# One fused transformer block: two PSUM bank sets for the last attention unit, and a new order of the steps before the router

## The reference

```python
h = layernorm(x) * (1 + ca) + sa
x = x + ga * attention(h)                       # causal, 16 heads
h = layernorm(x) * (1 + cb) + sb
scores = sigmoid(h @ gate_w.T)
topk_score, topk_ids = top_k(scores.T, 512)     # 16 experts over all 4096 tokens
eo = (silu(xin @ gw + gb) * (xin @ up + up_b)) @ down + down_b      # F = 1024
shared = (silu(h @ sh_gate) * (h @ sh_up)) @ sh_down                # SH = 512
x = x + gb * (scatter(eo * topk_score) + shared)
```

## Time and profile before

| | |
|---|---|
| median of 3 runs | 1237.21 us (1232.77 to 1240.11) |
| the profiled execution | 1228.18 us, its span 1226.5 us |
| mean granted clock of TensorE | 0.958 |
| busy: PE, DVE, POOL, ACT | 91%, 70%, 52%, 49% of the span |
| last unit of attention ends on PE | at about 447.9 us |
| first matmul of the experts | at about 629.8 us |

### The profile page before, as it was taken

The page is one execution under the profiler, slowest core; times in us unless marked ns, Lnnn a source line. Parts: engine busy times, 40 slices in busy tenths (PEclk is TensorE's granted clock), DMA queues, the critical chain, the costliest instruction groups (busy, mean ns, idle before and its releaser), DMA issues.

```text
span 1226.5 us, 21562 instructions
## 1 busy us (share of the span) xinstructions
PE 1120.3 (91%) x7422; PEld 875.4 (71%) x7422; DVE 858.3 (70%) x2174; ACT 600.0 (49%) x1085; POOL 642.5 (52%) x680
## 2 busy tenths in 40 slices
PE   4988988998898889999788999999999999999997
PEld 3545655555555457888677888888888888888886
DVE  5677797797786536778866776677776677776662
ACT  2247777776775563322143554444554444554441
POOL 4124476575573655222326666656666656666654
PEclk9679999999998789999999999999999999999998
DMA  5836768868778435875544445554545554556531
GB/s 168 104 51 112 110 123 169 168 134 173 142 141 161 140 104 181 205 202 145 159 127 116 144 123 159 126 133 116 145 124 158 126 130 119 145 122 160 126 87 18
DMA packets 100588, 165.46 MB, mean 135 GB/s; under 512 B 18680, under 2 KB 65272, under 8 KB 98432
## 3 DMA queue, kind: packets, MB, share of 16 engines
q1 hardware_dynamic: 84096, 137.86, 45.7%
q0 software_dynamic: 14336, 25.70, 10.9%
q10 hardware_dynamic: 2048, 0.53, 0.3%
HBM read 103.97 MB, written 34.13 MB: 113 GB/s over the span
## 4 chain that ended last, share of the span: by engine, by line
PE 34%; POOL 24%; issue 18%; DVE 9%; DMA 8%; SPq 3%; ACT 3%; ACTq 1%; POOLq 0%; DVEq 0%
POOL HTl L1642 12%; PE LB L761 6%; PE MB L761 6%; PE LB L505 4%; POOL out_y L1690 4%; PE MB L505 4%; POOL XG L1649 4%; DMA HT<-Us 3%; PE UB L505 3%; PE LB L598 3%; DVE junk L1167 3%; PE UB L614 2%; PE XB L505 2%; SPq L304 2%; DMA XT<-hD 2%
## 5 line engine op out<-in xcount | busy, mean ns | idle before, releaser
L1642 POOL TENSOR_TENSOR HTl<-HF,HTh 128x512 fp32r<-128x512 f32 x160 | 222.9, 1398 | 242.9 <-ACT HTh L973 242.7
L1167 DVE CUSTOM_DVE_ANT_0 junk<-MB,MK 128x256 bf16<-128x256 f32 (+3 forms) x512 | 219.8, 484 | 63.8 <-PE MB L575 62.4
L1553 POOL TENSOR_SCALAR_AFFINE_SELECT P<-P 128x256 f32<-128x256 f32 x256 | 101.4, 420 | 143.0 <-ACT P L913 143.0
L598 PE MATMUL LB<-QS,KS 50*128 50x256 f32 (+3 forms) x512 | 129.4, 372 | 16.2 <-ACT P L911 13.5
L973 ACT ACTIVATE HTh<-HF 128x512 fp32r<-128x512 f32 x160 | 100.4, 627 | 89.4 <-DVE HF L1429 89.4
L1690 POOL DMA_INDIRECT out_y<-EO,IDX x64 | 106.6, 1666 | 69.2 <-DVE EO L1516 63.7
L575 PE MATMUL MB<-KS,QS 48*128 48x256 f32 (+3 forms) x512 | 134.2, 377 | 8.0 <-DVE NM L1167 4.6
L911 ACT ACTIVATE P<-LB 128x768 f32<-128x768 f32 x128 | 103.8, 811 | 75.6 <-PE LB L598 75.1
L980 ACT ACTIVATE SIL<-LB,gbT 128x512 f32<-128x512 f32 x64 | 43.8, 685 | 185.4 <-PE LB L505 181.2
L598 PEld LDWEIGHTS LB<-QS,KS 50*128 50x128 f32 x512 | 83.2, 201 | 64.6 <-issue 46.5
L761 PE MATMUL LB<-WDh,HTh 128*128 128x256 f32 x320 | 94.3, 295 | 18.0 <-POOL HTl L1642 17.9
(11 more groups left out here) (265 smaller groups left out, 3011.1 us busy)
## 6 DMA issues: line engine op xcount, KB each, us to landing
WR<-in_gw SPq DMA_DIRECT2D x16, 1024.0 KB
WR<-in_uw SPq DMA_DIRECT2D x16, 1024.0 KB
WR<-in_dw SPq DMA_DIRECT2D x16, 1024.0 KB
QS<-ST SPq DMA_DIRECT2D x96, 128.0 KB, 4.8
KS<-ST SPq DMA_DIRECT2D x96, 128.0 KB, 5.9
hD<-h SPq DMA_DIRECT2D x8, 1024.0 KB, 5.5
XT<-hD SPq DMA_DIRECT2D x8, 1024.0 KB, 10.3
X<-in_x SPq DMA_DIRECT2D x8, 512.0 KB, 6.5
```

The lines of the kernel that those rows point to most:

```text
L598: m = e.matmul(LB[:, o:o + w], KS[base:base + 50, k, j * 128:(j + 1) * 128], QS[base:base + 50, k, 128 * j:512], start=True, stop=True)
L1167: m = e.tensor_tensor_reduce(junk[:, o:o + w], MB[:, o:o + w], MK[:, 512 - w:512], 1.0, -3e38, ALU.add, ALU.max, NM[:, k // 4, 4 * (k % 4) ...
L1553: m = e.affine_select(out=dd, in_=dd, compare_op=ALU.is_ge, fill=0.0, base=0, pattern=[[0, 2], [1, 128]], channel_multiplier=-1)
L1642: e.tensor_tensor(HTl[:, slot, :], HF[i][:], HTh[:, slot, :].bitcast(F32), ALU.subtract).then_inc(g_ht, 1)
```

## The change

1. In the last unit, odd heads use MB in place of LB (its maxima pass is over), so a head waits for the exp of the head two before.
2. SP issues the loads of the shared gate and up weights in unit 14 after head 1 (before: head 5), and their cuts on ACT and DVE go from unit 15, heads 2 to 5, to unit 14, heads 3 to 6.
3. Batch 6's output projection goes behind the last PV on PE and DVE. Its addition to X, batch 7's too, unit 15's normalise and low part, and the halves of shift2 for batch 6 (first half) and batch 7 (both) go from GpSimd to DVE.
4. On ACT, scale2 of batch 6 goes from before w = 0 to w = 2, behind unit 15's HNh. Batch 7's output projection and batch 6's h2T go to w = 3, batch 6's scores to w = 5, batch 7's h2T to w = 6 and its scores into the middle of w = 6, between the gate and the up matmuls.
5. The search starts at w = 7 instead of 10. SP spreads unit 15's inverses before it loads the down weight, and its stores follow the new order.

```diff
@@ -49,7 +49,7 @@
...
-W_TOPK = 10
+W_TOPK = 7
 W_PIECES = 42
...
@@ -392,7 +392,7 @@
...
                     stack(u + 2, 1)
-                if (u, k) == (NU - 2, 5):
+                if (u, k) == (NU - 2, 1):
...
@@ -427,10 +427,10 @@
...
         inverses(NU - 1)
+        spread_inverses(NU - 1)
...
         e.dma_start(WR[1][:, 0:1024].rearrange("p (k n) -> p k n", k=4), kn(sd)).then_inc(c_wr[1], 16)
-        spread_inverses(NU - 1)
         e.wait_ge(a_p, 2 * 8 * NU)
...
@@ -438,9 +438,9 @@
...
                 store_h2(NB - 2)
-            if w == 5:
+            if w == 4:
+                store_x2(NB - 1)
                 store_split(NB - 2)
-                store_x2(NB - 1)
             if w == 6:
...
@@ -455,9 +455,9 @@
...
                 load_gate_rows((w - 14) // 2)
-            if w == 4:
-                e.wait_ge(c_xd, 16 * (NB - 1))
+            if w == 8:
+                e.wait_ge(c_xd, 16 * NB)
                 e.dma_start(VR[:], cpos[:, 512:520]).then_inc(c_pos, 16)
...
@@ -586,16 +586,22 @@
...
         def main(u, k):
             base, n = 64 * (u % 2), n_head(u, k)
+            last = u == NU - 1
+            ps = MB if last and k % 2 else LB
+            if last and k == 1:
+                e.wait_ge(d_mx, 3 * 8 * NU)
+                e.wait_ge(a_nm, 2 * NU)
             if k % 4 == 0:
...
                     e.wait_ge(a_rows, 1)
-                elif j in (2, 0):
-                    e.wait_ge(a_p, 2 * (n - 1) + (2 if j == 0 else 1))
+                elif j in (2, 0) and not (last and k == 1):
+                    e.wait_ge(a_p, 2 * (n - (2 if last and k else 1)) + (2 if j == 0 else 1))
                 o, w = SPAN[j]
-                m = e.matmul(LB[:, o:o + w], KS[base:base + 50, k, j * 128:(j + 1) * 128],
+                m = e.matmul(ps[:, o:o + w], KS[base:base + 50, k, j * 128:(j + 1) * 128],
                              QS[base:base + 50, k, 128 * j:512], start=True, stop=True)
...
@@ -695,10 +701,12 @@
...
                         hT(b + 2, k - 5, ("hTa", "hTb")[k - 5])
-                    if k in (6, 7) and old:
+                    if k in (6, 7) and old and new:
                         outproj(b - 1, k - 6, ("outa", "outb")[k - 6])
...
         pv(NU - 1, 1, 1)
+        outproj(NB - 2, 0, "o0")
+        outproj(NB - 2, 1, "o1")
...
@@ -733,6 +741,14 @@
...
+        parts = [0]
+        def last_scores():
+            parts[0] += 1
+            if parts[0] == 2:
+                scores(NB - 1, "s0")
         def glu(n, m, wg, wu, xt, hook):
...
@@ -794,18 +810,17 @@
...
                 scores(NB - 3, "s2")
-            if w == 4:
+            if w == 3:
                 outproj(NB - 1, 0, "o0")
                 outproj(NB - 1, 1, "o1")
+                h2T(NB - 2, 0, "h1")
+                h2T(NB - 2, 1, "h0")
             if w == 5:
-                h2T(NB - 2, 0, "h0")
-                h2T(NB - 2, 1, "h1")
-                scores(NB - 2, "s0")
-            if w == 9:
-                h2T(NB - 1, 0, "h2")
-                h2T(NB - 1, 1, "h3")
+                scores(NB - 2, "s1")
+            if w == 6:
+                h2T(NB - 1, 0, "h0")
+                h2T(NB - 1, 1, "h1")
             if w == W_TOPK:
-                scores(NB - 1, "s1")
                 ticks[0] = -5
...
@@ -814,7 +829,7 @@
...
                     e.wait_ge(c_xt[b % 2], 16 * (b // 2 + 1))
-                glu(n_glu(b, i) - 1, i, shG, shU, XT[b % 2], tick)
+                glu(n_glu(b, i) - 1, i, shG, shU, XT[b % 2], last_scores if w == 6 else tick)
             else:
...
@@ -908,9 +923,10 @@
...
                 e.wait_ge(p_pv, (n - NP) // 4 + 1)
-            e.activation(P[n % NP][:, 512:1280], LB[:, 512:1280], ACT.Exp).then_inc(a_p, 1)
+            ps = MB if u == NU - 1 and k % 2 else LB
+            e.activation(P[n % NP][:, 512:1280], ps[:, 512:1280], ACT.Exp).then_inc(a_p, 1)
             e.wait_ge(p_mm, 2 * n + 2)
-            e.activation(P[n % NP][:, 0:512], LB[:, 0:512], ACT.Exp).then_inc(a_p, 1)
+            e.activation(P[n % NP][:, 0:512], ps[:, 0:512], ACT.Exp).then_inc(a_p, 1)
...
@@ -1047,27 +1063,27 @@
...
                         hT(b + 2, k - 5, ("hTa", "hTb")[k - 5])
-                if u == NU - 1 and 2 <= k < 6:
-                    cut(0, k - 2)
+                if u == NU - 2 and 3 <= k < 7:
+                    cut(0, k - 3)
         store_heads(NU - 1, 1)
         split_heads(NU - 2)
-        scale2(NB - 2, 0)
-        scale2(NB - 2, 1)
         for w, (kind, b, i) in enumerate(ORDER):
-            if w == 3:
+            if w == 2:
+                split_heads(NU - 1)
+                scale2(NB - 2, 0)
+                scale2(NB - 2, 1)
                 cut(1, 0)
                 cut(1, 1)
-                split_heads(NU - 1)
-            if w == 5:
-                h2T(NB - 2, 0, "h0")
-                h2T(NB - 2, 1, "h1")
-            if w == 6:
+            if w == 3:
+                h2T(NB - 2, 0, "h1")
+                h2T(NB - 2, 1, "h0")
+            if w == 4:
                 scale2(NB - 1, 0)
                 scale2(NB - 1, 1)
-            if w == 9:
-                h2T(NB - 1, 0, "h2")
-                h2T(NB - 1, 1, "h3")
+            if w == 6:
+                h2T(NB - 1, 0, "h0")
+                h2T(NB - 1, 1, "h1")
             if w == W_TOPK:
...
@@ -1284,7 +1300,7 @@
...
                         hT(b + 2, k - 6)
-                    if k == 7 and old:
+                    if k == 7 and old and new:
                         outproj(b - 1, 0, "outa")
...
@@ -1305,13 +1321,43 @@
...
                     e.tensor_tensor(GPl[:, :, 112:128], grv, GPh[:, :, 112:128].bitcast(F32), ALU.subtract).then_inc(d_gate, 1)
-                if u == NU - 1 and 2 <= k < 6:
-                    cut(e, 0, k - 2)
-        outproj(NB - 2, 1, "outb")
+                if u == NU - 2 and 3 <= k < 7:
+                    cut(e, 0, k - 3)
+        def add_x(b, i):
+            xs = X[:, b % 4, 2 * i:2 * i + 2, :]
+            e.wait_ge(d_tf, 2 * b + i + 1)
+            e.tensor_tensor(xs, xs, tf[:], ALU.add).then_inc(g_x2, 1)
+        def normalise(u):
+            e.wait_ge(c_us[0], 32 * (u + 1))
+            e.wait_ge(c_us[1], 32 * (u + 1))
+            e.wait_ge(c_hd[u % 2], 16 * (u // 2 + 1))
+            e.wait_ge(g_hn, u)
+            e.tensor_tensor(nf[:], HT[u % 2][:], DN[u % 2][:], ALU.mult).then_inc(g_nf, 1)
+        def split_heads(u):
+            e.wait_ge(a_hn, u + 1)
+            e.tensor_tensor(HNl[:, u % 2, :], nf[:], HNh[:, u % 2, :].bitcast(F32), ALU.subtract).then_inc(g_hn, 1)
+        def shift2(b, half):
+            ks = slice(2 * half, 2 * half + 2)
+            e.wait_ge(a_th, 2 * b + half + 1)
+            e.wait_ge(p_h2T, 2 * b)
+            e.wait_ge(c_tab, 16 * b)
+            kept(e.tensor_tensor(th[:, ks, :], th[:, ks, :], BT[b % 2][:, 2:3, :].broadcast_to([128, 2, D]), ALU.mult))
+            settled()
+            e.tensor_tensor(H2[:, ks, :], th[:, ks, :], BT[b % 2][:, 1:2, :].broadcast_to([128, 2, D]), ALU.add).then_inc(g_h2, 1)
+        outproj(NB - 2, 0, "o0")
+        add_x(NB - 2, 0)
+        outproj(NB - 2, 1, "o1")
+        inverses(NU - 1)
+        add_x(NB - 2, 1)
         stats2(NB - 2, 0)
...
         moments2(NB - 2)
-        inverses(NU - 1)
...
@@ -1431,33 +1477,31 @@
...
             if w == 1:
+                normalise(NU - 1)
+                split_heads(NU - 1)
                 scores(NB - 3, "s2")
-            if w == 3:
+            if w == 2:
+                shift2(NB - 2, 0)
                 cut(e, 1, 0)
                 cut(e, 1, 1)
-            if w == 4:
-                outproj(NB - 1, 0, "o0")
-                outproj(NB - 1, 1, "o1")
+            if w == 3:
+                for j in range(2):
+                    outproj(NB - 1, j, f"o{j}")
+                    add_x(NB - 1, j)
                 stats2(NB - 1, 0)
-            if w == 5:
-                h2T(NB - 2, 0, "h0")
-                h2T(NB - 2, 1, "h1")
-                scores(NB - 2, "s0")
                 stats2(NB - 1, 1)
                 moments2(NB - 1)
+                h2T(NB - 2, 0, "h1")
+                h2T(NB - 2, 1, "h0")
+            if w == 5:
+                shift2(NB - 1, 0)
+                shift2(NB - 1, 1)
+                scores(NB - 2, "s1")
             if w == 6:
-                e.wait_ge(a_th, 2 * NB - 1)
-                e.wait_ge(p_h2T, 2 * NB - 2)
-                e.wait_ge(c_tab, 16 * (NB - 1))
-                kept(e.tensor_tensor(th[:, 0:2, :], th[:, 0:2, :], BT[1][:, 2:3, :].broadcast_to([128, 2, D]), ALU.mult))
-                settled()
-                e.tensor_tensor(H2[:, 0:2, :], th[:, 0:2, :], BT[1][:, 1:2, :].broadcast_to([128, 2, D]),
-                                ALU.add).then_inc(g_h2, 1)
-            if w == 9:
-                h2T(NB - 1, 0, "h2")
-                h2T(NB - 1, 1, "h3")
+                h2T(NB - 1, 0, "h0")
+                h2T(NB - 1, 1, "h1")
+                scores(NB - 1, "s0")
```

(16 more changed lines are left out.)

## The result

The changed kernel is slower: 1245.62 us (median of 18 runs, 1238.34 to 1248.94) against 1232.67 us for the kernel before in the same session (18 runs, 1220.27 to 1240.11), a ratio of 1.011 (95% interval 1.0087 to 1.0133). A second session gave 1.0115 (1.007 to 1.0159). The profiled execution took 1245.97 us with a span of 1244.1 us. Forecast were 1239.0 us and "same". The forecast started from 1237.21 us, the median of three runs of the kernel before, and added some 2 us; against the 1232.67 us of 18 runs the change costs 13 us. So the miss is 11 us, and not the 6.6 that the two times suggest. The ratios leave out the few executions in a slower state, and differ from the quotient of the medians by up to 0.003.

The account below looks back on a forecast made before the run. PE was taken to bound the kernel, with under 12 us of removable idle time. Seven terms summed to +2.5 us on the profiled execution, 1239.7 us from the median, shaded to 1239; range 1231 to 1245 us.

Parts of the forecast that it names:

- Term 1: Unit 14: moving the shared gate and up weights' loads and cuts there costs +1.8 us; bounds 0.5 and 6.
- term 7: Low clock behind the new 2.75 us idle stretch before the last PV: +1.7 us; bounds 0 and 5.
- rival B: Slower: DVE and ACT in unit 14 stand behind a late WR (10.3 us landing): +9, 1246 us; chance 0.17.
- Term 2: Unit 15: with two bank sets, scores no longer wait for the previous head's exp: -0.4 us.
- Term 3: End of unit 15: batch 6's output projection behind the last PV leaves PE idle 2.75 us there: +2.4 us.
- Term 4: Before w2: SIL ahead of scale2 on ACT removes a 2.5 us wait and 1.7 us of low clock: -4.2 us.
- Term 5: Shared stage from w1: the order by need removes 2.6 us of waits and adds 5.6: +3.0 us; bounds 2.5 and 8.
- rival C: In w1: DN lands quickly, at 456.8, so added waits fall from 5.6 to about 3.3: 1237.4 us, "same"; chance 0.2.
- Term 6: Top-k search three steps earlier: HTl wait gone, tail net -0.4, gather's wait unchanged: -1.8 us.

Follow-up runs that it names:

- f1: Changed kernel with 60 unused matmuls in three PE waits (last PV, batch 6's first h2T, gather): 1236.92 us, against 1243.0 us for the changed kernel.
- g1: Changed kernel with VectorE's two down-weight cuts moved behind batch 6's h2T: 1242.37 us, 1.0098 of the kernel before.
- g2: Kernel before with only the two bank sets of the last unit added: ratio 1.0032 (0.9999 to 1.0066) to the kernel before.
- e3: Changed kernel with batch 6's output projection put back into heads 6 and 7 of unit 15: 1240.73 us, 1.0089 of the kernel before.
- e4: Changed kernel with three parts undone (search at w10, cuts in unit 15, projection in heads 6 and 7): 1236.04 us, 1.0036 of the kernel before.
- h2: Kernel before with unused matmuls in four PE waits (first SIL, PT, w40's up matmuls, gather): ratio 0.9999 (0.9967 to 1.0031).
- i1: Kernel before with the change's WR loads in unit 14, cuts two heads later than the change's: ratio 1.0040 (1.0013 to 1.0066).

## Why the prediction was wrong, point by point

The means of the two traces of each kernel, against the terms as they were put. The sum agrees within 1 us between two traces of a kernel; the single rows are rough, with up to 6.6 us between two traces:

| stretch | terms | forecast | measured |
|---|---|---|---|
| unit 14 | 1 | +1.8 | +6.8 (27.45 against 20.7) |
| unit 15 to w0 | 2, 3, 7 | +3.7 | +3.4 (30.05 against 26.7) |
| w0 to expert 0 | 4, 5, 6 | -3.0 | +3.5 (188.8 against 185.3) |
| experts | none | 0 | -0.1 |
| sum | | +2.5 | +13.4 |

**Term 1 failed, and most: +6.8 us where it had +1.8.** The place and the chain were right: WR late, ACT at the first cut, DVE behind it, PE at the transpose of the maxima. The size was not, for two reasons. The first is the time at which the loads go out, which was put "right behind the HT transfer of head 1", 6.7 us after unit 14's first exp (404.3 less 397.6). The waits in front of these loads, above all that for the last stack DMAs (`c_stack`), were not priced; WR lies in part on the space from which these read. The second is the low clock, for which the term had nothing. SP's rows of the second trace of the changed kernel show it:

```profile
401.81 1.87 SPq L304 DMA_DIRECT2D KS<-ST  x3
406.86 0.51 SPq L314 DMA_DIRECT2D HT<-Us  x1
410.53 0.39 SPq L400 DMA_DIRECT2D WR<-in_sg  x1
```

SP is through with HT at 407.4, waits 3.0 us for the last KS transfer and issues WR 3.2 us behind HT. In seven of the ten traces with this edit it stood 1.9 to 3.4 us there. In the other three, the first trace of the changed kernel, f1 and g1, the gap is 0.2, but HT itself was 0.7 to 2.0 us later. The loads left 7.6 us (408.98 less 401.4) and 9.3 us after that exp. The landing itself, 5 us in my sum, was 5.8 us. So the first cut came 13.3 and 15.1 us after unit 14's first exp, against 12.0 forecast. In unit 14 PE is idle 6.3 and 7.7 us in the two traces, against 3.2 and 2.5 before: +4.1 on the mean, near the 1.8 plus the 1.3 and 3.1 us by which the cut was late. The clock (counted as under term 7) cost 7.0 and 4.7 us there, against 5.1 and 1.7, which is +2.5, though chance is as large in it. The lower bound of the term, a landing in 3.7 us, stood on no row; the eight traces in which ACT waited for WR have 5.8 to 6.7. This is the mechanism of rival B, which had 0.17, but not its cause (a transfer of 8 us or more), and that its 1246 met the measured time is luck: it was +9 on a start 4.5 us too high, where +13 was measured, a good part of it behind unit 14. The Trainium skill's fit (DMA: Bandwidth & Descriptors, "Anatomy of one DMA"), made for GpSimd's path, would have put WR at 4.4 us as an estimate; the 5.8 us of SP's two loads are above it.

**Term 2, right.** Unit 15 hardly moves with the bank sets alone (g2).

**Term 3, right; term 7, right in its first part.** PE idles 2.65 us before the last PV (2.75 forecast), and the clock, at 1.00 in the 2.5 us ahead of this wait, falls with it, costing 2.1 us in that PV alone (4.49 less 2.36) where 1.7 stood for the stall. By the ratios e3 takes back 2.6 us.

**Term 4, right.** The wait for SIL is gone.

**Term 5, too low.** DN was used 4.05 us after its issue, between the 5.6 of the sum and the 2.65 of rival C; and still PE waited 4.7 and 0.7 us at tf, where I had 2.3 and 0.9. The chain on DVE was taken at 0.69 us an operation. The two pieces of shift2 took 1.73 and 1.65 us, while GpSimd did its own half in the same time. The low clock behind this wait was only in the bounds of term 7. From w0's to w10's first gate matmul PE takes 46.5 and 47.1 us, against 44.1 and 44.3, so terms 4 and 5 together are +2.6 instead of -1.2.

**Term 6, half right, and the second failure.** The HTl wait at w11 went (w10 to w12 takes 6.2 us instead of 7.5: -1.4, as forecast), PT's 2.4 and tb's 3.3 came where and as large as put. From w12 to w42 the changed kernel takes 102.7 and 102.9 us, the one before 103.3 and 110.0, the last by low clock. But "the gather for expert 0 stays at w42 and its wait stays" is wrong: it went from 3.5 to 7.84 us, and with the low clock behind it w42 to expert 0 takes 33.8 and 32.2 us instead of 27.0 and 26.9. I had moved VectorE's instructions and not looked at which of SP's transfers wait for them (GBt, XL, the store of `out_y`), and what meets the gather when they go out.

**Term 7, too small as a whole, and the third failure.** It charged the clock for one stall. Adding up (1 - clock) times PE's busy time over windows of 1 us, from w0 to expert 0, the clock cost 10.8 and 8.5 us in the changed kernel, 5.1 and 9.7 us in the one before. Of the mean difference of 3.5 us there, 2.3 is idle time and 2.3 the clock, less 1.1 of busy time elsewhere. The spread within one kernel is as large as the difference, so that single traces don't give the clock's share; f1's timed runs do, with 6 us for the clock behind its three places.

**What stays open.** e4's remainder of 0.0036 (it may be anything from 0.0003 to 0.0069) has no single step shown for it; the two bank sets, which it contains, gave 0.0032 (-0.0001 to 0.0066) alone. i1's 0.0040 has no stall in its trace that explains it. That the store of `out_y` lengthens the gather was not tested by moving it.

## What to carry to other kernels

When a load is moved ahead, price its own waits first: it can go no earlier than the last reader of the space it lands in, and the engines that stand in front of its data stop in order. When an engine's list is moved, follow which DMA issues wait for that list, and which large transfers then go out together with a small one that somebody waits for. And charge each long wait of PE with the low clock behind it: in this kernel every one of 2.6 us or more between w0 and expert 0 had it. Where such a wait can't be removed, a dozen unused matmuls in it can be cheaper than leaving it empty, as in f1; h2 shows that it need not be. Last, take two traces of a kernel before pricing a stretch of it.

## What the runs showed of the hardware

- The time goes with the granted clock from run to run. Over 133 runs of the kernel before, in five sessions, the mean clock went from 0.948 to 0.973 and the time from 1218.87 to 1241.61 us, with a correlation of -0.75, about 7 us per 0.01. The large waits behind w0 agree within 0.7 us between two traces of a kernel, except that for XT (1.0 and 2.7 us before); the falls of the clock don't. The Trainium skill (TensorE: Matmul & The Clock Gate, "What's actually happening") says that one kernel shows a different number of slow matmuls from run to run. It says so of the start of a kernel; the traces show the same in the middle of one (0.77 and 0.91 in unit 14 of the kernel before).
- Between w0 and expert 0 the 18 traces have 41 waits of PE of 2.6 us or more, and in or behind each of them the clock goes to 0.50. Of the 27 between 1.9 and 2.5 us about half have it: the one for PT (2.1) has none behind it in the first trace of the kernel before, and has it in the second.
- Filling a wait of 2.65 us with ten matmuls brought the PV behind it from 4.49 to 2.36 us. In an already tuned kernel (h2) the same did not show in the time.
- The two loads of WR (1 MB in all) took 5.8 to 5.9 us from the first issue to the first cut in seven traces of kernels where ACT stood waiting for them, and 6.7 in one.
- The last piece of the indirect gather was used 3.7 to 4.0 us after its issue in eleven traces, and 6.8 to 7.5 us in the seven where a store of 512 KB was issued within 0.1 us of it, with loads of 128 and 512 KB behind.
- DVE's 128x512 float32 additions and products, 0.69 us alone, took 1.65 and 1.73 us beside GpSimd's (1.29 and 1.61 us).
